# A planned four-part kernel: more places for the second group of expert tiles, three fused or halved operations, and a new plan

## What is computed

```
xn = layernorm(x)
x  = x + mamba(xn) + moe(xn)                  # layer 0
xn = layernorm(x)
x  = x + geodesic(xn) + local_layers(xn)      # layer 1
```

## Time and profile before

| | |
|---|---|
| time, median of 3 runs | 2499.11 us (2494.23 to 2502.01) |
| profiled execution: time, span | 2502.13 us, 2500.8 us |
| mean granted TensorE clock | 0.842 of 2.4 GHz |
| instructions | 32678 |
| HBM read, written | 111.33 MB, 12.85 MB |

### The profile page before, as it was taken

One profiled execution on the slowest core, in us unless ns is written; L12 is line 12 of the kernel. 1 busy time (PEld: TensorE's weight loads), 2 busy tenths in 40 slices (PEclk: granted clock), 3 DMA queues, 4 the chain that ended last, 5 costly groups with the idle time before them and its releaser, 6 DMA issues.

```text
span 2500.8 us, 32678 instructions
## 1 busy us (share of the span) xinstructions
PE 1993.4 (80%) x10866; PEld 1328.3 (53%) x10866; DVE 1930.0 (77%) x3005; ACT 1833.5 (73%) x2759; POOL 525.0 (21%) x206
## 2 busy tenths in 40 slices
PE   4777778888678878878787888878787878888867
PEld 2544546775345555655465555655455555655645
DVE  5788895545997889699867889699968889674554
ACT  3436868697669677887777787887678786978883
POOL 2413121022112121302212121302112211221220
PEclk8787878999887888888787989888687989776778
DMA  7631112432211110111001110111001010000000
GB/s 250 222 98 56 51 34 67 131 116 85 83 42 53 46 35 18 40 35 55 22 13 48 39 48 13 40 46 53 13 31 39 32 53 1 1 1 5 1 1 5
DMA packets 67527, 126.29 MB, mean 51 GB/s; under 512 B 8836, under 2 KB 40132, under 8 KB 67236
## 3 DMA queue, kind: packets, MB, share of 16 engines
q1 hardware_dynamic: 61808, 113.19, 13.9%
q0 software_dynamic: 2816, 7.21, 0.8%
q10 hardware_dynamic: 2740, 3.80, 0.4%
HBM read 111.33 MB, written 12.85 MB: 50 GB/s over the span
## 4 chain that ended last, share of the span: by engine, by line
PE 31%; DVE 30%; ACT 18%; issue 16%; DMA 2%; SPq 1%; POOL 1%; DVEq 0%; ACTq 0%; POOLq 0%
PE ps L763 6%; DVE hB L1434 5%; PE ps L984 4%; PE ps L942 4%; DVE hB L1428 3%; DVE hB L1440 2%; PE ps L1068 2%; ACT arena L1255 2%; ACT arena L1331 2%; PE ps L1043 2%; DVE arena L1506 2%; DVE n_c L1513 2%; ACT L758 2%; PE ps L1103 2%; DVE lss L1568 2%
## 5 line engine op out<-in xcount | busy, mean ns | idle before, releaser
L1726 POOL TENSOR_TENSOR arena<-arena 128x2048 f32<-128x2048 f32 x64 | 297.5, 4649 | 1188.9 <-ACT arena L1257 1188.8
L763 PE MATMUL ps<-w_ident,arena 128*128 128x128 f32 x1647 | 301.1, 319 | 123.6 <-ACT arena L1331 43.7
L942 PE MATMUL ps<-hB,w_ident 128*128 128x512 f32 x512 | 303.4, 725 | 75.3 <-DVE hB L1440 75.2
L763 PEld LDWEIGHTS ps<-w_ident,arena 128*128 128x128 f32 x1647 | 227.7, 166 | 234.1 <-issue 139.1
L1434 DVE TENSOR_TENSOR_SCAN hB<-dA,hB 128x1024 f32<-128x1024 f32 x128 | 324.6, 2539 | 9.1 <-ACT dA L1219 8.8
L1730 POOL TENSOR_TENSOR arena<-arena,rb 128x1024 f32<-128x1024 f32 x64 | 151.9, 2374 | 574.6 <-DVE rb L1566 574.6
L1219 ACT ACTIVATE dA<-dtv,w_A_log 128x510 f32<-128x510 f32 x256 | 168.8, 718 | 109.6 <-DVE hB L1434 108.6
L1043 PE MATMUL ps<-w_l_wqkv,arena 128*128 128x512 f32 x384 | 212.5, 677 | 33.7 <-DVE lss L1568 15.5
L1506 DVE TENSOR_SCALAR arena<-ps 128x512 f32<-128x512 f32 x256 | 163.8, 681 | 63.6 <-PE ps L984 62.8
L1331 ACT ACTIVATE arena<-ps,nmx 128x128 f32<-128x128 f32 (+1 forms) x512 | 158.9, 397 | 65.5 <-DVE nmx L1588 64.8
L942 PEld LDWEIGHTS ps<-hB,w_ident 128*128 128x128 f32 x512 | 106.3, 229 | 181.9 <-issue 116.2
(11 more groups left out here) (198 smaller groups left out, 4216.3 us busy)
## 6 DMA issues: line engine op xcount, KB each, us to landing
BC<-bc_d SPq DMA_DIRECT2D x128, 512.0 KB, 3.7
BC<-in_experts SPq DMA_DIRECT2D x31, 514.0 KB, 3.3
arena<-in_experts SPq DMA_DIRECT2D x15, 514.0 KB, 3.6
arena<-in_x SPq DMA_DIRECT2D x8, 256.0 KB, 5.8
xnT_d<-arena SPq DMA_DIRECT2D x8, 256.0 KB, 3.7
hB<-xnT_d SPq DMA_DIRECT2D x8, 256.0 KB, 2.6
x<-in_x SPq DMA_DIRECT2D x8, 256.0 KB, 2.9
out<-go SPq DMA_DIRECT2D x8, 256.0 KB, 2.3
```

What stands on the lines that cost most here:

```text
L763: return t.transpose(out_, in_, ident[0:k, 0:k])
L942: e = t.matmul(lb(), ident, hB[k % 2][:, j], start=q == 0 and j == 0, stop=q == NQ - 1 and j == NG - 1)
L1726: g.tensor_tensor(la[m % 2], la[m % 2], cl, ALU.subtract).then_inc(g_sub, 1)
```

## The change

1. Group 1 of the expert tiles gets six places for weights, b2 and rows and three for transposed rows, hidden values and results (`NW`, `ND`). The four mamba tensors `xs`, `zs`, `dtv`, `du` become one tensor `mv`, in which places 3 to 5 lie. So tile 15 still waits for the scans of pair 1, and tile 18, the first in `mv`, waits for the output product of pair 1 (`p_mo`).
2. The mask goes into PSUM in one product of 320 columns for a head and not in two of 128 and 192.
3. The two clamps of a pair of heads become one instruction of 128x1024 over two banks, and `g_score` must get neighbouring banks.
4. `g_sub` is two instructions of 128x1024, and the next block's clamp waits only for the half that it overwrites.
5. The plan: new costs for three kinds, new due times, a shift for each stream and pair (`STREAM`), so that all five orders are new.

```
+
+NW, ND = [3, 6], [2, 3]
...
-SWITCH = 67.0
-
-LATER = {...}
+SWITCH = 62.0
+
+LATER = {...}
+
+STREAM = {...}
...
-        unit(t0, ("e_load", j), ("e_scat", q), *[("e_down", j - 3) for z in range(1) if j >= 3],
-             *[("e_xt", j - 2) for z in range(1) if j >= 2],
-             *[(u, 1, 0, STEPS - 1) for u in ("m_sum", "m_hc") if q])
-        unit(t0, ("e_xt", j), ("e_load", j))
-        unit(t0, ("e_up", j), ("e_xt", j), *[("e_down", j - 2) for z in range(1) if j >= 2])
-        unit(t0, ("e_down", j), ("e_up", j), *[("e_store", j - 2) for z in range(1) if j >= 2])
+        t0 = 20 + 2.7 * (j - GJ[q]) + (FIRST + SECOND - 40) * q
+        unit(t0, ("e_load", j), ("e_scat", q), *[("e_down", j - NW[q]) for z in range(1) if j >= GJ[q] + NW[q]],
+             *[("e_down", GJ[1] - 1) for z in range(1) if j == GJ[1]],
+             *[(u, 1, 0, STEPS - 1) for u in ("m_sum", "m_hc") if q], *[("m_out", 1) for z in range(1) if j >= GJ[1] + 3])
+        y = j - ND[q]
+        unit(t0, ("e_xt", j), ("e_load", j), *[("e_up", y) for z in range(1) if y >= GJ[q]])
+        unit(t0, ("e_up", j), ("e_xt", j), *[("e_down", y) for z in range(1) if y >= GJ[q]])
+        unit(t0, ("e_down", j), ("e_up", j), *[("e_store", y) for z in range(1) if y >= GJ[q]])
         unit(t0, ("e_store", j), ("e_down", j))
     unit(2, ("m_weights",))
...
 
-EARLY, FIRST, SECOND, PERIOD = 49.0, 120.0, 105.0, 239.0
...
 
-        if unit[0] != "score":
...
-        xs = sb("xs", [P, CH, T])
-        zs = sb("zs", [P, CH, T])
-        dtv = sb("dtv", [P, CH, T])
-        du = sb("du", [P, CH, T])
+        mv = sb("mv", [P, 4 * CH * T])
+        xs, zs, dtv, du = [mv[:, k * CH * T:(k + 1) * CH * T].rearrange("p (c t) -> p c t", c=CH) for k in range(4)]
...
-        a2, a3 = Arena(BC), Arena(hB_)
...
         for x_, y_ in ((a0, a0), (a2, a3)):
-            wE.append([x_.get(EW) for _ in range(3)])
-            b2E.append([x_.get(DM) for _ in range(3)])
-            xt.append([x_.get(DM) for _ in range(2)])
-            xtT.append([y_.get(P) for _ in range(2)])
-            hE.append([y_.get(FJ, P) for _ in range(2)])
-            ye.append([y_.get(DM) for _ in range(2)])
+            q = len(wE)
+            wE.append([(x_ if k < 3 else a4).get(EW) for k in range(NW[q])])
+            b2E.append([(x_ if k < 3 else a4).get(DM) for k in range(NW[q])])
+            xt.append([(x_ if k < 3 else a4).get(DM) for k in range(NW[q])])
+            xtT.append([y_.get(P) for _ in range(ND[q])])
+            hE.append([y_.get(FJ, P) for _ in range(ND[q])])
...
-                        for z in range(2):
-                            cols = slice(P, SC) if qt else slice(0, P)
-                            t.matmul(lb(z)[:, cols], ident_b[:], mask_b[:, cols], start=True, stop=False)
                         for z in range(2):
                             q_ = qT[head_rows(z), k, b * L + qt * P:b * L + (qt + 1) * P]
                             o_, j0 = (lb(z)[:, P:SC], WIN) if qt else (lb(z)[:, 0:P], 0)
-                            e = t.matmul(o_, q_, kT[head_rows(z), k, b * L + j0:b * L + (L if qt else P)], start=False, stop=True)
+                            e = t.matmul(o_, q_, kT[head_rows(z), k, b * L + j0:b * L + (L if qt else P)], start=False, stop=qt == 1)
                     e.then_inc(p_sc[b], 1)
                     for z in range(2):
                         read_by(unit, a_e[b], 4 * n + k + 1, z)
...
-                        v.tensor_scalar(cl[:, 2 * (k % 2) + z], lb(z), -1.0 + 1e-7, 1.0 - 1e-7, ALU.max, ALU.min).then_inc(v_gs, 1)
+                    v.tensor_scalar(cl[:, 2 * (k % 2):2 * (k % 2) + 2], two_banks(unit), -1.0 + 1e-7, 1.0 - 1e-7,
+                                    ALU.max, ALU.min).then_inc(v_gs, 1)
                 elif u == "g_av":
                     m = BLOCKS * i + HB * b + k
                     hs = slice(k * HB, (k + 1) * HB)
...
                 elif u == "g_sub":
-                    m = BLOCKS * i + HB * b + k
+                    m = BLOCKS * i + HB * b + k // 2
+                    half = slice(2 * (k % 2), 2 * (k % 2) + 2)
                     g.wait_ge(a_ln, m + 1)
-                    g.tensor_tensor(la[m % 2], la[m % 2], cl, ALU.subtract).then_inc(g_sub, 1)
...
+                        s.wait_ge(d_scat[q], 16 * (1 + TT * (GP[q + 1] - GP[q])))
                     if i == GJ[1]:
 
                         s.wait_ge(p_ys, 2 * STEPS)
-                    if i >= 3:
-                        s.wait_ge(p_y, i - 2)
-                        s.wait_ge(v_y, i - 2)
-                    if i >= 2:
-                        s.wait_ge(p_xt, i - 1)
+                        s.wait_ge(p_y, GJ[1])
+                    if i == GJ[1] + 3:
+                        s.wait_ge(p_mo, 2)
+                    z = weights_in(i)[0]
+                    if i - GJ[q] >= NW[q]:
+                        s.wait_ge(p_y, i - NW[q] + 1)
+                        s.wait_ge(v_y, i - NW[q] + 1)
                     e = s.value_load(exi[0:1, i:i + 1], min_val=0, max_val=NE - 1)
-                    s.dma_start(wE[q][i % 3], d["experts"][bass.ds(e, 1)].rearrange("a p f -> p (a f)")).then_inc(d_wE[i % 3], 16)
-                    s.dma_start(b2E[q][i % 3], d["b2"][bass.ds(e, 1)].rearrange("a p f -> p (a f)")).then_inc(d_wE[i % 3], 16)
-                    s.dma_start(xt[q][i % 2], xs_d[q][(i - GJ[q]) * P:(i - GJ[q] + 1) * P]).then_inc(d_xt[i % 2], 16)
+                    s.dma_start(wE[q][z], d["experts"][bass.ds(e, 1)].rearrange("a p f -> p (a f)")).then_inc(d_wE[z], 16)
+                    s.dma_start(b2E[q][z], d["b2"][bass.ds(e, 1)].rearrange("a p f -> p (a f)")).then_inc(d_wE[z], 16)
+                    s.dma_start(xt[q][z], xs_d[q][(i - GJ[q]) * P:(i - GJ[q] + 1) * P]).then_inc(d_wE[z], 16)
                 elif u == "e_store":
```

133 lines of the change are left out of this document (79 added, 54 removed).

## The result

The changed kernel takes 2457.82 us (median of four executions, 2456.92 to 2467.65), the kernel before on the same chip 2498.81: a ratio of 0.9844, 95% interval 0.9821 to 0.9866. The forecast was 2461 us. The total is right within 4 us, but by luck: its parts are not right, and most of what follows is about that.

The account below looks back on a forecast made before the run. No engine was full and the bound differed by stage, TensorE in tiles and tail, VectorE in pair 2's scans. Terms -12 -13 -2 -2 -3 -6 = -38 gave span 2463, forecast 2461 us, own range 2435 to 2485.

Parts of the forecast that it names:

- VectorE's 20 to 35 us: Whole kernel: the prediction called itself wrong if VectorE's busy time didn't fall by 20 to 35 us.
- the chain is on VectorE for 30%, and I give it that share: Clamps and halves: VectorE time saved was counted at 30%, giving -3 and -6 us.
- the halves' term: GpSimd's subtraction in halves: shorter holds save 19 us of VectorE, counted as -6 us of span.
- rival 1: Holds and waits, tail and middle: they shrink more and the masks' 22 us all count; 2430 us, chance 0.14.
- The term of -3: Clamps in one instruction: 10 us less VectorE work, priced at -3 us of span.
- The moved units, -12: Second group's tiles and scans of pair 2: together 339 us against 351 after moving units, -12 us.
- the tail, -13: Behind the last scan: 284 TensorE units and not 291, and cheaper masks, make the stretch 13 us shorter.
- rival 3: Second tile group: tiles keep 6.8 us each for a reason that isn't TensorE; 2517 us, slower, chance 0.10.
- "-2" for the **middle: The middle, 736 to 2128 us: 11 more TensorE units, +12, against cheaper masks, -14, make -2 us.
- rival 4: Middle and tail: the new orders chain worse, +20 and +19 us; 2512 us, chance 0.10.
- The term per product: Mask products on TensorE: one of 320 columns takes 250 ns, saving 85 ns each, 22 us in all.
- The new wait of tile 18: SyncE's queue: tile 18's load waits for pair 1's output product; cost 0, or some 5 us once.

Follow-up runs that it names:

- whole_sub: The changed kernel with GpSimd's subtraction in one instruction again; ratio to the kernel before 0.9933.
- short_sub: The changed kernel with each half of the subtraction done for only 32 of 512 columns, the rest left out; ratio to the kernel before 0.9322.
- quarters: The changed kernel with the whole subtraction in four GpSimd instructions of 128x512 a block; ratio to the kernel before 0.9618.
- fine_pieces: The changed kernel with subtraction in eight instructions of 128x256 a block and the rotation's addition in four; 2370.39 us, ratio to the kernel before 0.9485.
- two_clamps: The changed kernel with two clamps of 128x512 again, both banks handed on after the second; ratio to the kernel before 0.9849.
- three_places: The changed kernel with three places for weights and two for results in the second tile group, orders planned anew; ratio to the kernel before 0.9957.
- plan_places: The changed kernel's plan and places with two mask products, two clamps and one whole subtraction again; ratio to the kernel before 1.0126.
- two_masks: The changed kernel with the mask again in two products of 128 and 192 columns; ratio to the kernel before 0.9954.
- old_masks: The kernel before, own plan and places, with only the mask in one product; ratio to the kernel before 0.9930.
- old_plan: The kernel before, own plan, places and clamps, with one mask product and the subtraction in halves; ratio to the kernel before 0.9856.
- old_halves: The kernel before with only the subtraction in halves and the finer wait of the next clamp; ratio to the kernel before 0.9898.
- small_pieces: The changed kernel with each subtraction half as four instructions of 32 columns, the rest left out; ratio to the kernel before 0.9331.

## Why the prediction came out, and which of its steps were wrong

The total came within 3 us by luck: two errors cancelled, as the sum at the end of this section shows. Of the signs that the prediction named, the stage of the tiles (146 us, VectorE at 42%), the scans of pair 2 (187), the mask product (252 ns), the clamp (1.2 us) and the longest hold of a scan (4451 - 2282 ns = 2.2 us) came out; the lower means of L1434 and L1440 and VectorE's 20 to 35 us did not.

**The step that failed: "the chain is on VectorE for 30%, and I give it that share".** With the plan of the change kept and only GpSimd's instructions varied, VectorE's busy time goes from 1947.4 (whole_sub) to 1799.8 us (short_sub) and the span from 2482.4 to 2331.5: 150.9 us of span for 147.6 of VectorE, 1.02 for 1. The kernels between lie near that line; the one furthest off is quarters, with 50.4 us of span for 39.1. Held time comes off the span in full and not at three tenths. With 1 for 0.3 the halves' term would have been -19 and not -6; -22 were measured. I had a hint in hand, VectorE at 85% of the middle in the earlier trace rows, and even had it as rival 1, but priced the term by the chain's share, which is an average over stages and says nothing on what happens if one engine's time shrinks everywhere. In the middle VectorE's busy time goes from 1209 (whole_sub) to 1096 us (short_sub) and the stage from 1415 to 1303: VectorE's idle time there stays at 206 us. It is 208 before, 211 in the change, 211 in fine_pieces and 195 in quarters. So the microseconds come off one for one; at an unchanged share of 0.85 they would come off 1.18 for one. Why the idle time stays no run here tells. One thing goes along that no run separates: from whole_sub to short_sub TensorE's busy time falls too, from 1943.4 to 1892.9 us, at a clock of 0.849 and 0.874.

The clamp limits that rule: 10 us more of VectorE's busy time (two_clamps) cost nothing measurable. An earlier free bank isn't the reason, since that edit hands on both banks together; the reason is open. The term of -3 can't be told from 0 here.

**The moved units, -12, and the tail, -13.** As stage lengths they held, the sizes off: tiles and scans -19, tail -29. The rule behind them (a stage takes its units at the same share of busy time) gave 155 + 184 for a measured 146.1 + 186.6, and 202 for 196 in three_places. The tiles come every 146.1 / 31 = 4.7 us, so rival 3 fell. But these stages are not where the change gets its time. What failed is "-2" for the **middle**: in plan_places it takes 46 us more, and new plan and places alone make the kernel 31 us slower. The plan lets GpSimd's instructions meet the scan steps more often: 45 us more held in three groups, for which the order gives no hint if one counts units per engine only. This is the middle's half of rival 4, with twice its price of 20 us (the rival's own working, 1392 x 0.02, is 28, and a fall from 85 to 84% is 17). The tail, which that rival made longer, got shorter. In the change itself the operations hide it, and the middle reads +7.

**The tail's size.** TensorE is busy 269.6 us there and not 299.7 - 11, at a granted clock of 0.82 and not 0.78. I had carried the old clock over. two_masks has the clock at 0.78 and a tail of 355.4 us, old_masks has 359.8 and plan_places 358.0: of the 29 us some 14 are the plan's and 12 the mask product's.

**Masks.** The term per product was right (252 against 250 ns, 21 us against the earlier trace rows for a forecast of 22). The effect was 27 us in the new plan, 18 at a like clock, 17 alone in the old plan, 10 on top of the halves (0.9898 to 0.9856, with intervals that touch). TensorE's other products take longer when the mask takes two, in executions with a lower clock: 67 us of busy time for the mask's own 24 from the change to two_masks (clock 0.850 and 0.835), but 31.5 for 22 from old_plan to old_halves (0.849 and 0.851). What comes first, the clock or the crowding, these runs don't tell. The estimate from the Trainium skill's figures ("TensorE: Matmul & The Clock Gate", "Back-to-back issue gap") was 16 us; the groups have 21 to 24, so the trace's rows were the nearer source. Rival 1's sum takes 6 us more for the masks, but 21 of their 22 us stand in the forecast already: 7 + 18 + 1 = 26 us, and it is 2435 us and not 2430.

**Places, SyncE's queue, tables.** The new wait of tile 18 costs nothing, as forecast: no wait for the output product (L1780) shows in SyncE's queue, and in the timeline that product ends at 380.1 us, while the queue issues the load of tile 17 up to 383.5 and goes on with tile 18 at 384.2. The places alone were not isolated. ScalarE's two more table loads were not isolated either.

**The sum.** Split by what they rest on, the forecast's terms are -12, -9 and +12 for units in other places (-9) and -14, -5, -2, -3 and -6 for masks, clamps and halves (-30). The runs have +31 for plan and places, and -70 from there for the three operations, together -39. Two errors, an overrated plan and underrated operations, cancelled to 3 us. Undone one by one, the operations are worth 22, 27 and 0, which is some 50 and not 70: 20 us show only when all are gone. From plan_places the first of the two that count gains 43 (halves, two_masks) or 48 us (mask, whole_sub; both with the one clamp), the second 27 or 22. The intervals of the four ratios don't cover that, and its cause is open. So is why the new plan meets more holds; a plan that counts them was not made.

## What to carry to other kernels

If an engine that is as busy in the longest stage as VectorE is here (85%) has means well above the shortest duration of the same shape, try that excess as span in full, as it was here, and look for who holds it; then cut the holder's instructions down, even if it works longer for it, as long as it has room. Don't credit a new instruction order from counts of units per stage: compare the means of the groups that can be held, and run the plan without its companions, since here it cost 31 us that two small edits hid. Don't carry a stage's clock over when its content changes: the tail's went from 0.78 to 0.82. Before a profiled execution is compared with another, compare both with the times and clocks of all executions of their kernels.

## What the runs showed of the hardware

- A GpSimd tensor instruction holds a VectorE instruction with two SBUF inputs to its own end, and is itself held: GpSimd's half block has a median of 2366 ns and a mean of 2805 in the change. The Trainium skill, "GPSIMD Engine Reference", table of specifications, names the shared interface; the trace agrees and adds the lengths, 3.02 and 4.43 us where 1.21 and 2.28 are undisturbed. The clamp, which reads PSUM, was not held once: its 128 instructions in the change take 1192 to 1227 ns.
- The grain of the turn is one instruction. With pieces of 128x2048, 128x1024, 128x512 and 128x256 for the subtraction, and at the last also for the addition, the three scan groups lose 136, 116, 88 and 45 us, and GpSimd's whole busy time is 546, 594, 671 and 824 us. The longest scan takes 6.59 us with 128x2048, 4.45 with 128x1024 and 2.82 with 128x256, that is 4.3, 2.2 and 0.5 over the undisturbed 2.28.
- GpSimd's instructions by size, undisturbed (median) and with their waits for VectorE (mean): 128x64 322 ns, and 505 (small_pieces) or 638 (short_sub); 128x256 730, and 871 or 1052; 128x512 1279, and 1715; 128x1024 2366, and 2805; 128x2048 4526, and 4649. Eight of 128x256 take 5.8 us undisturbed for one of 4.5; the larger part of what they add in busy time is waiting.
- Two bf16 products of 128 and 192 columns in place of one of 320 raised TensorE's busy time by 67 us, 43 more than their own, with the mean granted clock at 0.835 and not 0.850; at 0.851 and 0.849 (old_halves and old_plan) it was 31.5 us, 10 more than their own.
- The mean granted clock differs between executions of one kernel, and the time goes with it: 0.844 to 0.849 with 2475 to 2477 us and 0.832 to 0.839 with 2480 to 2497 us in two_masks.
